# Asking for the tokens first in each iteration, and a new written-out order for the steps of two interleaved chains

## The reference, cut to what matters

```
x = x + xattn0(ln(x), ctx)        # 16 heads, each with its own 16 of the 257 context rows
x = x + attn0(ln(x))              # causal, scores from 3-d distances
x = x + moe(ln(x))                # shared expert, and the best 2 of 8 experts for each token
x = x + xattn1(ln(x), ctx)        # causal self attention, attention on the context, 256-1024-256 MLP
x = x + diff_attn(ln(x))          # 32 x 32 attention among the heads of a token, MLP
x = x + product_keys(ln(x))       # 16 x 64 scores for a token, top 16 of each, top 16 of the sums
```

## Time and profile before

| | |
|---|---|
| median of 3 runs | 3512.15 us (3507.14 to 3529.97) |
| the profiled execution's own time | 3509.67 us |
| its span, from first to last instruction | 3507.8 us |
| mean granted TensorE clock | 0.856 of full speed |
| busy: TensorE, VectorE, ScalarE, GpSimd | 2613.3, 1927.4, 937.8, 667.4 us |
| DMA | 392.64 MB, mean 112 GB/s |

### The profile page before, as it was taken

How to read it: one execution, slowest core, us unless ns; L and a number is a source line. 1 busy time by engine, 2 the same in 40 slices (tenths; PEclk the granted TensorE clock), 3 DMA queues, 4 the chain that set the end, 5 groups by cost and what they waited for, 6 DMA issues and landing times. The chain is left out here.

```text
span 3507.8 us, 47305 instructions
## 1 busy us (share of the span) xinstructions
PE 2613.3 (75%) x16384; PEld 1863.9 (53%) x16384; DVE 1927.4 (55%) x7470; ACT 937.8 (27%) x2008; POOL 667.4 (19%) x572
## 2 busy tenths in 40 slices
PE   5786898478884898758986689847898489876543
PEld 3574576255762567535664457625585256742421
DVE  3314564844847447664558556475384644674458
ACT  1212342123321233222421234212332124212210
POOL 0101132112312114021140112211130211402040
PEclk9897999689996999978998799968999699985766
DMA  6274163231523236040441416322261324503100
GB/s 227 73 258 154 41 207 105 98 115 65 200 84 107 85 103 225 26 156 31 153 175 37 152 57 202 113 105 88 78 213 62 116 72 135 193 29 110 25 0 6
DMA packets 211639, 392.64 MB, mean 112 GB/s; under 512 B 83344, under 2 KB 163472, under 8 KB 186160
## 3 DMA queue, kind: packets, MB, share of 16 engines
q1 hardware_dynamic: 205232, 372.49, 30.7%
q0 software_dynamic: 6144, 16.79, 1.4%
HBM read 350.55 MB, written 38.67 MB: 111 GB/s over the span
## 5 line engine op out<-in xcount | busy, mean ns | idle before, releaser
L796 PE MATMUL ps<-xbT,stream 128*128 128x128 f32 x2560 | 342.8, 291 | 12.3 <-ACT xbT L1122 6.1
L796 PEld LDWEIGHTS ps<-xbT,stream 128*128 128x128 f32 x2560 | 327.7, 205 | 36.3 <-issue 15.0
L299 POOL TENSOR_TENSOR hTB<-pb,sbuf 128x2048 f32<-128x2048 f32 x32 | 151.9, 4757 | 427.0 <-DVE pb L1656 427.0
L607 PE MATMUL ps<-cmat,aTB 128*128 128x512 f32 x256 | 159.4, 781 | 60.6 <-DVE sbuf L1740 56.9
L599 PE MATMUL ps<-ident,xnB 128*128 128x128 f32 x256 | 56.8, 341 | 163.8 <-DVE xnB L1285 127.5
L510 POOL DMA_INDIRECT hTA<-y_slots,slot x64 | 62.9, 982 | 606.6 <-DMA y_slots<-yb 589.6
L470 POOL TENSOR_TENSOR rstdA<-veA,mhalf 128x4 f32<-128x4 f32 x24 | 24.4, 1017 | 789.5 <-DVE veA L1278 789.5
L1013 PE MATMUL ps<-ident,work 128*50 128x128 f32 x32 | 12.5, 392 | 216.4 <-DVE work L1795 216.4
L809 PE MATMUL ps<-stream,hTA 128*128 128x256 f32 x640 | 163.6, 402 | 0.6 <-ACT yb L1143 0.6
L796 PE MATMUL ps<-xbT,ctxA 128*128 128x128 f32 x1280 | 157.4, 276 | 2.0 <-DMA ctxA<-in_experts 1.9
L796 PEld LDWEIGHTS ps<-xbT,ctxA 128*128 128x128 f32 x1280 | 151.4, 192 | 11.1 <-DMA ctxA<-in_experts 5.0
(11 more groups left out here) (277 smaller groups left out, 6001.0 us busy)
## 6 DMA issues: line engine op xcount, KB each, us to landing
stream<-in_experts SPq DMA_DIRECT2D x88, 1024.0 KB, 5.2
stream<-in_experts SPq DMA_DIRECT2D x88, 512.0 KB, 6.0
ctxA<-in_experts SPq DMA_DIRECT2D x40, 1024.0 KB, 5.1
work<-in_ctxT SPq DMA_DIRECT2D x32, 1028.0 KB, 6.9
hTB<-in_ctxN SPq DMA_DIRECT2D x32, 1024.0 KB, 6.9
down<-in_experts SPq DMA_DIRECT2D x40, 512.0 KB, 6.0
ctxA<-in_ctxT SPq DMA_DIRECT2D x16, 1024.0 KB, 8.8
stream<-in_ctxT SPq DMA_DIRECT2D x16, 1024.0 KB, 11.0
```

Source lines behind the costliest of these rows:

```text
L299: return e.tensor_tensor(out.rearrange("p (a d h) -> p a d h", a=8, d=16), a.unsqueeze(2).broadcast_to([P, 8, 16, 16]), vals[:, t, :].rear ...
L607: ins = mm(out, aT[:, k, t * P:(t + 1) * P], wt[:, k, cols], start=k == 0, stop=k == KT - 1)
L796: ins = mm(ps[:, 2 * (b % 2) + u, f * P:(f + 1) * P], wu[:, u, k, f * P:(f + 1) * P], xbT[:, b % 2, k, :], start=k == 0, stop=k == KT - 1)
```

## The change

1. The tokens of group g were asked for by one DMA of 512 KB in the front's first step on SyncE, which in `ORDER` stood behind five steps of the back, the first of which issues the back's context loads. Now four DMAs of 128 KB, one for each tile, are issued before either chain's first step, each with a semaphore of its own (`x_in0` to `x_in3`), and VectorE waits for each ahead of that tile's statistics. `before_h1` does its waits once, as it did.
2. `ORDER` is a new string, with the same 68 f and 130 b.

```diff
 ORDER = (
-    "bbbbbfbfbfbbbfbbfbbfbffbfbfffbfbfbfbfbbbfbbfbfbffbffbfbffbbbfbfbfbbfbbfbfbbbbbffbfbffbbfbfbfbfbb"
-    "fbfbbffbbfbfbfbfbbfbfbfbbfbbfbffbbfbbbbfbbbbbbbbbbbbbbbbfbbffbbbbbbfbbbfbbbbfbbbbfbbbbbfbbbbbfbb"
-    "bbbfbb")
+    "bbbbfbfbbbfbfbbbfbfbffbfbffbfbbffbfbfbbbfbbfbbffbfbfbfbffbffbbbbfbfbfbfbbbbbfbffbffbbfbbfbfbbbfb"
+    "ffbbfbfbbfbffbbfbffbbbfbfbbfbfbfbbbbbfbfbbbbbbbbbbbbbbbfbbbfbfbbbbbbbbbbbffbbfbfbfbbbfbbbbbbbbbb"
+    "bbbbff"
+)
...
+        x_in = [sems["x_in%d" % t] for t in range(T)]
...
                     rows = bass.ds(g * P, P)
+                    if "f" in streams:
+                        for t in range(T):
+                            sp.dma_start(xA[:, t, :], dram["x"][rows, t * D:(t + 1) * D]).then_inc(x_in[t], 16)
...
-                        sp.dma_start(xA, dram["x"][rows, :].rearrange("p (t d) -> p t d", t=T)).then_inc(x_in, 16)
...
-                        if before:
-                            before()
                         for t in range(0 if early else T):
+                            if before:
+                                before(t)
                             if t == 0 and V.n:
                                 own_steps()
                             vv.bn_stats(st[:, t, :], src[:, t, :]).then_inc(vec_done, V.step(tag, "st", t))
...
-                        yield from norm("n0", xA, xnA, smallA, before=lambda: v.wait_ge(x_in, 16))
+                        yield from norm("n0", xA, xnA, smallA, before=lambda t: v.wait_ge(x_in[t], 16))
...
-                        def before_h1():
-                            v.wait_ge(pe_done, PE["xpv", T - 1])
-                            wait_scaled(v, "z", T - 1)
+                        def before_h1(t):
+                            if t == 0:
+                                v.wait_ge(pe_done, PE["xpv", T - 1])
+                                wait_scaled(v, "z", T - 1)
```

More of the change, by code:

```diff
@@ L214, in build @@
         u50 = work[:, 1400:1400 + 2 * NP].rearrange("p (s n) -> p s n", s=2)
-        names = ["pe_done", "vec_done", "act_done", "pool_done", "w_in", "x_in", "ctxA0", "ctxA1", "ctxB0", "ctxB1",
+        names = ["pe_done", "vec_done", "act_done", "pool_done", "w_in", "x_in0", "x_in1", "x_in2", "x_in3", "ctxA0", "ctxA1", "ctxB0", "ctxB1",
                  "ctxN0", "ctxN1", "ctxl_in", "gu0", "gu1", "gu2", "dn0", "dn1", "dn2", "out_done", "late_in",
@@ L220, in build @@
         pe_done, vec_done, act_done, pool_done = (sems[n] for n in names[:4])
-        w_in, x_in, ctxl_in, out_done, late_in = (sems[n] for n in ("w_in", "x_in", "ctxl_in", "out_done", "late_in"))
+        w_in, ctxl_in, out_done, late_in = (sems[n] for n in ("w_in", "ctxl_in", "out_done", "late_in"))
+        x_in = [sems["x_in%d" % t] for t in range(T)]
         n_late = 16 * (len(load_layout()) - len(EARLY) + 2)
```

## The result

The kernel is faster by 2.8%: 3415.18 us (median of 4 runs, 3409.75 to 3425.92) against 3510.19 for the kernel before (4 runs on the same chip, 3507.14 to 3529.97). The ratio is 0.972, with a 95% interval from 0.968 to 0.977. The profiled execution took 3419.78 us with a span of 3417.7. TensorE's mean granted clock is the same in both profiles, 0.852 and 0.856 before.

What follows compares the result with a forecast made beforehand. No engine bounds the kernel throughout: TensorE and VectorE wait for each other or are both near full, by stage. Eight terms summed to -8.4 us an iteration, times 7 is -59, giving 3451 us from 3509.67; range 3420 to 3507.

Steps and rivals of the forecast that it cites:

- the statistics of `y3`: From the second attention to these statistics: waits of TensorE hidden by MLP matmuls and long steps, -2.5 us an iteration.
- `h1`: Up to its scaling: router work leaves VectorE's chain of three norms, which gets shorter, -1.2 us an iteration.
- the tail: End of the iteration: VectorE's wait of 1.44 us for the matmuls of a "hid" goes, -1.4 us an iteration.
- b76 to b94: Around the second MLP to the first product keys: moved block work only partly fits waits, +2.2 us an iteration.
- the loss: Projections to combining of the scores: `shared(3)` and block 0's up matmul make TensorE late, +3.8 us an iteration.
- the tokens: Iteration start to the queries' matmul: asked for earlier, VectorE's wait of 3.37 us goes, -2.5 us an iteration.
- the stretch before `h2`: From combining the scores to scaling `h2`: TensorE work moves out and VectorE waits less, -4.9 us an iteration.
- b12 to b20: Context attentions up to the first MLP: waits filled by front steps, less two new waits, -1.9 us an iteration.
- more than forecast: Rival: TensorE doesn't hold up the scores, so +3.8 becomes 0; -12.2 us an iteration, 3424 us, chance 0.1.
- The rival of the projections at the low clock: TensorE idles ahead of the transposes of `h1`, slowing work behind: +18.3 us an iteration, 3579 us, chance 0.08.
- The one of blocks at the low clock in the tail: Bunched blocks run slow, VectorE waits 8.1 us an iteration: 3507 us, chance 0.2 including other ways waits return.

Runs made afterwards that it cites:

- `sh3_back`: The changed kernel with `shared(3)` moved back into the wait ahead of the transposes of `h1`: 3387.10 us, ratio 0.967.
- `up0_later`: The changed kernel with the up matmul of block 0 moved back behind the first scores: 3414.19 us, ratio 0.975.
- `seg3_only`: The kernel before with the four token DMAs first and only f34 to f49 in their new places: 3453.85 us, ratio 0.986.
- `x_only`: The changed kernel with the old order, so only the four token DMAs first are new: 3476.98 us, ratio 0.989.
- `seg4_only`: The kernel before with the four token DMAs first and only f50 to f64 in their new places: 3448.53 us, ratio 0.980.
- `x_one`: `sh3_back` with the tokens in one 512 KB DMA at the same place in the queue: 3380.38 us, ratio 0.962.

## Why the prediction was right, and where it was wrong

The sign holds, and three of the eight terms hold within 0.3 us: the statistics of `y3`, `h1` and the tail. The sum was 6.8 us an iteration too small, 48 us in all. Three terms make it so: b76 to b94 (3.9 too high), the loss (3.1) and the tokens (1.4). Two err the other way: the stretch before `h2` brings 3.6 of the 4.9, and b12 to b20 measured 1.0 of the 1.9, which the old order has too. There the new waits of 0.9 and 1.9 were expected to leave a gain, and by the first MLP none is left beside the tokens.

*The term of +3.8, "the loss".* The mechanism was right and its parts were mis-sized. From the scaling of `h1` the first score comes 4.9 us later, where I had 5.65. `shared(3)`'s share, forecast at 3.7, is 5.0 by `sh3_back`, and made otherwise than I wrote: its work of 3.6 comes behind the transposes while only 0.8 is won ahead of them, and 2.7 are the clock of the projections. That the up matmul of block 0 was on the path was wrong: `up0_later` takes its 1.85 us away from the first score and the combining stays. And I let the pairs of scores give back 1.85 us by looking at one wait of 2.25; behind the first score there are three such waits in iteration three, 3.99 us together on average, and all of them go. From the first score to the combining it is 4.2 us shorter, in the changed kernel and in `seg3_only` alike. 4.9 - 4.2: 3.8 became 0.7. An error in one part hid one in the other.

*The term of +2.2 from b76 to b94.* It measured -1.7. I counted f56 between ScalarE's copies as 2.3 us of work that fits only in part, +1.3, and f57 as +0.5: each as work against a hole, with the MLP and the product keys behind it at the durations of the old rows. The hole was forecast well, 0.95; but the first half of the MLP behind it is 1.2 shorter, so f56 is -0.25. f55 ahead of b78 costs nothing (forecast 0.4): the transposes of `h2` start as long behind the scaling as before. f57 makes the transposes of `n5` 0.3 later, but from there to the end of the first product keys' matmuls it is 1.7 shorter, so it is -1.4 where I had +0.5. The window of the earlier trace rows had a clock of 0.93 there, and I looked for the clock only where it could fall. This is the step that failed most, 3.9 us an iteration. Part of it could have been luck of the first profile; it isn't: this stretch is 1.7 shorter in six of the seven kernels with both steps moved and f56 in the hole (1.1 in `seg4_only`), and in the five other profiles with the old places it lies from 0.8 under to 0.4 over that of the kernel before.

*The tokens, -2.5.* It measured -3.9, and `x_only` says the same, 3.95. The wait goes whole. The row that groups the statistics, of the kernel before and of the changed one:

```profile
L1273 DVE BATCH_NORM_STATS2 stA<-xA 128x6 f32<-128x256 f32 x32 | 11.2, 414 | 29.6 <-DMA xA<-in_x 29.6
```

```profile
L1276 DVE BATCH_NORM_STATS2 stA<-xA 128x6 f32<-128x256 f32 x32 | 11.4, 416 | 6.8 <-DMA xA<-in_x 6.0
```

The 6.0 is that of the front alone, where the kernel before waited 6.95, so (29.6 - 6.95) / 7 = 3.2 go in each of the seven iterations. I had taken off 0.85 for the statistics standing ahead of b4, and that isn't seen. The four issues take 3.80 us of SyncE's queue in iteration three, not the estimated 1.9:

```profile
1085.45 3.80 SPq L334 DMA_DIRECT2D xA<-in_x  x4
```

The first context load is asked for 5.5 us into the iteration on average, where it was 2.1 before and is 2.7 in `x_one`. That `x_one` is no clearly faster shows that this delay costs next to nothing. The clock of this stage went from 0.59 to 0.67 in the windows, which may be the other 0.7; that is not settled.

Of the rivals, "more than forecast" (3424) is the nearest by its time, but not by what it said: TensorE does hold up the first scores, and they are made good afterwards. That its number for the loss, 0, came so near is luck. The rival of the projections at the low clock, forecast for 18.3 us with a chance of 0.08, is true in small: these matmuls take 13.1 us without `shared(3)` (16.68 - 3.60) where they took 12.1. It is bounded, since the clock is back before they end: the eight matmuls behind the first 24 take 3.60 us, as at full speed. The one of blocks at the low clock in the tail did not come: line 799 takes 1.95 us there, and the block of 3.45 to 3.65 us that each iteration had before is gone. The Trainium skill (TensorE: Matmul & The Clock Gate, HAM oscillation) has waits between bursts make each burst begin at the low clock. The trace agrees in part: the two windows at 0.50 and 0.72 begin so, but behind the same waits 22 of 49 second MLPs began at 1.00. I had weighed it for the tail alone, where TensorE's work got shorter and the time gained only what was forecast without it.

The other page of the Trainium skill that I weighed (DMA: Bandwidth & Descriptors, Bandwidth) is neither borne out nor contradicted: it says that small transfers lower the rate, and no reader here waited on the rate (3384.73 against 3380.38 us).

What stays open: why the gains of single stretches don't add up to that of the whole order; why one empty hole brings the low clock and the next doesn't; what f57 does by itself; and how much of the 3.9 at the tokens is clock. `sh3_back` is the best of the orders run, 0.967 (0.964 in its second run, and 0.962 [0.958, 0.966] beside it with one request). In one of the seven iterations of its first profile TensorE's first score comes 16.8 us behind the down matmuls instead of 12.9, and there ScalarE waits for the relay, 6.42 and 2.17 us ahead of its last two groups:

```profile
464.80 3.30 ACT L1206 ACTIVATE work<-hTB,diag 128x256 f32<-128x256 f32 x8 [6.42 <-DMA hTB<-qk_rows]
470.53 1.70 ACT L1206 ACTIVATE work<-hTB,diag 128x256 f32<-128x256 f32 x4 [2.17 <-DMA hTB<-qk_rows]
```

So the relay is late next there; in the second profile two iterations are like that, and one in `x_one`.

## What to carry to other kernels

When one engine has both short dependent steps and long blocks, what stands right ahead of a long block also decides at which clock the block begins. Here a step of 2.3 us in such a wait kept the clock up in every iteration, worth 1.7 us wherever the low clock would have come and 0.9 on average; a step of 3.7 us taken out of one cost 5.0. A filled wait with other waits around it (the projections of the kernel before) didn't do. So carry the clock through a stage, not the old durations. And where two engines hand work to and fro in a row of equal steps, sum the waits of the whole row instead of pricing one of them (4.0 us here, where one was 2.25), but take apart what the sum mixes: a wait that only moved to another line, and a part of the program that the change doesn't touch.

## What the runs showed of the hardware

The same instructions of the front alone take from 274 to 297 us; where two profiles were laid side by side the granted clock differed (0.85 against 0.58 in one window). That is up to 0.7% of this kernel, so one profile's total can't be compared with another's to better than that; points within the iteration, averaged over seven, agreed within 1.6 us in two profiles of one kernel, and within 3.7 in equal stretches of different kernels. A wait of TensorE of 2.47 us ahead of eight short transposes was followed by projections of which the first 6 us ran at 0.50; with the same transposes and the same last wait of 0.90 behind work without a break, they ran at 1.00. Behind waits of 0.97 to 1.10, 0.29 and 0.90 us, 32 matmuls of the same kind took 14.00 us in some iterations and 15.70 in others of the same kernel.
